# A transformer layer in five phases: the order of two interleaved stages, and the loop of an output projection, written anew

## What is computed

```python
def _layernorm(x, eps=1e-5):
    m = mean(x); v = var(x)
    return (x - m) / sqrt(v + eps)

# attention, x of 4 x 4096 x 2048, 16 heads of 128, latent size 512
q = x @ Wq + bq
kv_latent = x @ Wdown
k, v = kv_latent @ Wk_up, kv_latent @ Wv_up
q, k = rope(q), rope(k)
ctx = softmax(causal(q @ k.T / sqrt(128))) @ v
attn = ctx @ Wo + bo

x = x + _layernorm(attn(_layernorm(x)))
x = x + _layernorm(ffn(_layernorm(x)))     # ffn: silu(x Wg) * (x Wu), then Wd, int8 weights
```

## Time and profile before

| | |
|---|---|
| median of 3 runs | 6407.89 us (6402.77 to 6916.29) |
| the profiled execution: its time | 6408.3 us |
| its span, slowest core (core 4) | 6406.7 us |
| the eight cores' spans | 6387.0 to 6406.7 us |
| mean granted TensorE clock, core 4 | 0.851 |
| busy share of TensorE matmul, VectorE, ScalarE, GpSimd | 69%, 25%, 21%, 13% |

### The profile page before, as it was taken

How to read it: one execution, slowest core, us unless ns; L and a number is a source line. 1 busy time by engine, 2 the same in 40 slices (tenths; PEclk the granted TensorE clock), 3 DMA queues, 4 the chain that set the end, 5 groups by cost and what they waited for, 6 DMA issues and landing times.

```text
span 6406.7 us, 67363 instructions; the slowest of 8 cores (6387.0 to 6406.7 us)
## 1 busy us (share of the span) xinstructions
PE 4390.4 (69%) x20979; PEld 2018.1 (32%) x21376; DVE 1584.5 (25%) x2965; ACT 1347.2 (21%) x3067; POOL 819.8 (13%) x924
## 2 busy tenths in 40 slices
PE   0254544775666666533338998699986999879986
PEld 0011111333433333311113443244432444334432
DVE  0334352443333333233331110211102110021101
ACT  0222321115666666511110000001001000010000
POOL 0112121340000000000001111111111111111111
PEclk9877777886777677766669999899998999989998
DMA  9343435317777787754339994699848996499944
GB/s 184 107 124 110 124 93 135 82 57 163 151 150 147 152 154 150 146 146 135 126 105 161 154 151 129 154 151 151 148 128 158 149 154 130 127 167 155 151 122 134
DMA packets 1566328, 883.21 MB, mean 138 GB/s; under 512 B 777122, under 2 KB 1541026, under 8 KB 1550242
## 3 DMA queue, kind: packets, MB, share of 16 engines
q0 software_dynamic: 679296, 434.14, 39.6%
q1 hardware_dynamic: 839842, 327.28, 23.0%
q10 hardware_dynamic: 46848, 117.45, 5.6%
HBM read 398.53 MB, written 109.05 MB: 79 GB/s over the span
## 4 chain that ended last, share of the span: by engine, by line
PE 44%; DMA 19%; DVE 11%; ACT 10%; issue 10%; POOL 3%; SPq 2%; ACTq 1%; DVEq 0%; POOLq 0%
PE ps L1051 14%; PE ps L1065 14%; PE ps L1118 8%; DMA arena<-wd 7%; ACT arena L786 7%; PE ps L884 4%; DMA ctxr<-xin 3%; DMA arena<-arena 2%; PE ps L758 2%; DVE smalls L780 2%; POOL arena L641 2%; PE ps L719 1%; DVE arena L481 1%; DMA arena<-wo 1%; DMA x_scr<-arena 1%
## 5 line engine op out<-in xcount | busy, mean ns | idle before, releaser
L1051 PE MATMUL ps<-arena 128*128 128x512 bf16 x4015 | 929.4, 382 | 270.7 <-DMA arena<-wg 143.8
L1118 PE MATMUL ps<-arena 128*128 128x512 bf16 x4014 | 912.1, 380 | 145.1 <-DMA arena<-wd 139.8
L1065 PE MATMUL ps<-arena 128*128 128x512 bf16 x4013 | 919.7, 379 | 4.4
L786 ACT ACTIVATE arena<-ps,smalls 128x512 bf16<-128x512 f32 (+1 forms) x1152 | 748.5, 667 | 460.7 <-DVE smalls L780 314.9
L758 PE MATMUL ps<-arena 128*128 128x512 bf16 (+1 forms) x1073 | 455.0, 484 | 412.2 <-ACT arena L786 325.0
L1051 PEld LDWEIGHTS ps<-arena 128*128 128x128 bf16 x4096 | 402.7, 98 | 757.9 <-issue 281.0
L446 PE MATMUL ps<-arena 128*128 128x512 bf16 x1004 | 329.2, 472 | 397.2 <-DVE arena L481 197.5
L1118 PEld LDWEIGHTS ps<-arena 128*128 128x128 bf16 x4096 | 386.8, 98 | 669.8 <-issue 238.3
L1081 DVE TENSOR_SCALAR ctxr<-ps,smalls 128x512 bf16<-128x512 f32 x256 | 192.1, 750 | 1501.1 <-PE ps L1065 1501.1
L1065 PEld LDWEIGHTS ps<-arena 128*128 128x128 bf16 x4096 | 400.9, 98 | 483.2
L1076 ACT ACTIVATE ctxr<-ps,smalls 128x512 bf16<-128x512 f32 x256 | 176.0, 687 | 1562.5 <-PE ps L1051 1562.4
(11 more groups left out here) (74 smaller groups left out, 2742.6 us busy)
## 6 DMA issues: line engine op xcount, KB each, us to landing
arena<-wg POOLq DMA_DIRECT2D x128, 1024.0 KB, 6.8
arena<-wu POOLq DMA_DIRECT2D x128, 1024.0 KB, 7.1
arena<-wd POOLq DMA_DIRECT2D x256, 512.0 KB, 3.8
ctxr<-xin SPq DMA_DIRECT2D x32, 1024.0 KB, 6.7
arena<-wo_scr ACTq DMA_DIRECT2D x16, 2048.0 KB, 9.3
xnf_scr<-arena SPq DMA_DIRECT2D x16, 1024.0 KB, 11.8
k_scr<-ctxr SPq DMA_DIRECT2D x16, 1024.0 KB, 7.9
v_scr<-ctxr SPq DMA_DIRECT2D x16, 1024.0 KB, 7.2
```

The lines of the kernel that those rows point to most:

```text
L786: s.activation(P_b[par][:, n0:n0 + N], psa[:, 0:N], ACT.Exp, bias=negc[:, par:par + 1], scale=1.0, accum_out=lacc[:, par * 8 + ci: par * 8 ...
L1051: rr = t.matmul(ga, wg_s[slp][:, fc, icw * 128:(icw + 1) * 128], x1nfm[:, fc, :], start=(fc == 0), stop=(fc == NH - 1))
L1065: rr = t.matmul(ua, wu_s[slp][:, fc, icw * 128:(icw + 1) * 128], x1nfm[:, fc, :], start=(fc == 0), stop=(fc == NH - 1))
L1118: rr = t.matmul(psa, f_b[:, quar * 4 + ic, j * 128:(j + 1) * 128], wd_s[qp][:, ic, :], start=(quar == 0 and ic == 0), stop=(quar == 15 and ...
```

## The change

Two parts. In phase A the generators are no longer drawn in turn: for each kg the whole of `front(kg+1)` is recorded, then the whole of `back(kg)`.

In phase D Wo is loaded once, whole, into `wo_all` (four 2 MB loads at the start). The tile of 128 tokens is now the outer loop, and the four og the inner one; the row work of a tile stands right behind its four sums. `att` becomes two buffers of one tile. The transposed context `ctxfm` has one buffer instead of two: the four transposes of the next block are recorded behind the matmuls of a block's last tile. In `ln_soup` the last step, which applies scale and shift, goes from DVE to ACT, and needs a small POOL product before it (`nmr`).

```diff
-        fr = front(0)
-        run_all(fr)
-        fr = front(1) if NKG > 1 else iter(())
+        run_all(front(0))
         for kg in range(NKG):
-            bk = back(kg)
-            while True:
-                try:
-                    next(bk)
-                except StopIteration:
-                    break
-                try:
-                    next(fr)
-                except StopIteration:
-                    pass
-            run_all(fr)
-            fr = front(kg + 2) if kg + 2 < NKG else iter(())
+            if kg + 1 < NKG:
+                run_all(front(kg + 1))
+            run_all(back(kg))
...
-        ctxfm = [cd.take([NH, 512], BF16) for _ in range(2)]
-        wo_s = [cd.take([NH, 512], BF16) for _ in range(2)]
-        att = cd.take([4, DM], F32)
+        ctxfm = cd.take([NH, 512], BF16)
+        wo_all = cd.take([NH, DM], BF16)
+        att2 = [cd.take([DM], F32) for _ in range(2)]
...
+        woevs = []
+        for og in range(4):
+            def fnw(s, og=og):
...
+                return s.dma_start(wo_all[:, :, og * 512:(og + 1) * 512], sap)
+            woevs.append(st("S", fnw, dma="dA"))
+        s_wo.produced(woevs)
...
-        for ttb in range(4):
-            tp = ttb % 2
-            if ttb + 1 < 4:
-                cfm_load(ttb + 1)
-
+        for tt in range(16):
+            tp = tt % 2
+            att = att2[tp]
+            s_att = s_att2[tp]
+            j4 = tt % 4
...
             for og in range(4):
...
+                bank = og % 2
...
+            if j4 == 3 and tt + 1 < 16:
+                cfm_load(tt // 4 + 1)
...
-                    e9 = st("V", lambda v: v.tensor_scalar(
-                        dst_ap, src_ap, nmean, rstd, op0=ALU.add, op1=ALU.mult),
-                        waits=[e8] + prod_waits(sD))
+                e8b = st("G", lambda g: g.tensor_mul(nmr, nmean, rstd),
+                         waits=[e8])
+                e9 = st("S", lambda s, src_ap=src_ap, dst_ap=dst_ap:
+                        s.activation(dst_ap, src_ap, ACT.Identity,
+                                     bias=nmr, scale=rstd),
+                        waits=[e8b] + prod_waits(sD))
```

More of the change, by code:

```diff
@@ L833, in build_program @@
         bo_s = cd.take([DM], F32)
-        s_cfm = [Slot(), Slot()]
-        s_wo = [Slot(), Slot()]
-        s_att = Slot()
+        s_cfm = Slot()
+        s_wo = Slot()
+        s_att2 = [Slot(), Slot()]
         s_xt = [Slot(), Slot()]
@@ L844, in build_program @@
         s_bo.produced(st("Q", lambda q: q.dma_start(bo_s, bob), dma="dQ"))
+        woevs = []
+        for og in range(4):
+            def fnw(s, og=og):
+                sap = bass.AP(wo_scr.tensor, og * 512,
+                              [[DM, 128], [128 * DM, NH], [1, 512]])
+                return s.dma_start(wo_all[:, :, og * 512:(og + 1) * 512], sap)
+            woevs.append(st("S", fnw, dma="dA"))
+        s_wo.produced(woevs)
         def cfm_load(ttb):
-            tp = ttb % 2
             tevs = []
@@ L850, in cfm_load @@
                 tt = ttb * 4 + j
-                ev = st("Q", lambda q, tt=tt, j=j, tp=tp: q.dma_start(
-                    ctxfm[tp][:, :, j * 128:(j + 1) * 128],
+                ev = st("Q", lambda q, tt=tt, j=j: q.dma_start(
+                    ctxfm[:, :, j * 128:(j + 1) * 128],
                     ar_view(ctxr, 0, [NH, DM], BF16)[:, tt, :],
@@ L855, in cfm_load @@
                     waits=cons_waits(s_ctx) +
-                    (prod_waits(s_cfm[tp]) if j == 0 else []), dma="dQ",
+                    (prod_waits(s_cfm) if j == 0 else []), dma="dQ",
                     xpose=True)
@@ L859, in cfm_load @@
                 s_ctx.used(ev)
-            s_cfm[tp].produced(tevs)
+            s_cfm.produced(tevs)
         cfm_load(0)
-        for ttb in range(4):
-            tp = ttb % 2
-            if ttb + 1 < 4:
-                cfm_load(ttb + 1)
-            for og in range(4):
[L869 to L944, removed]
-                    e9 = st("V", lambda v: v.tensor_scalar(
-                        dst_ap, src_ap, nmean, rstd, op0=ALU.add, op1=ALU.mult),
-                        waits=[e8] + prod_waits(sD))
[L948 to L973, removed]
```

86 lines of the change are left out of this document (added).

## The result

The kernel after is slower: its time is 1.015 of that before, with a 95% interval of 1.010 to 1.021, so whether the loss reaches 2% stays open. Its profiled execution takes 6500.9 us (span 6499.4, core 3) where that of before takes 6408.3; the forecast was 6524, within 6488 to 6566. A phase starts where the table says; for D and E that is the first load that SP issues for it.

The account below looks back on a forecast made before the run. Phases A and D were taken to be bound by chains of waits, with no engine near full. From 6408.3 us, +150 for A and -34 for D gave 6524 us, 1.8% more, range 6488 to 6566.

Parts of the forecast that it names:

- Phase A, the period: Phase A: front and back add up, so the period is 131.8 us instead of 110.9, and A costs +150 us.
- if every front's first load costs more behind v than behind k: Phase A, upper bound: allows 1.7 us more per period for a front's first load behind the store of v.
- The third latent group: Phase A, back: TensorE starts this group at the low clock, 5.6 us; if warm, each period is 2.2 shorter.
- Phase D: Whole of phase D: gains from the new tile order outweigh a later start and block-end stalls, -34 us.
- start of the phase to the first reduce: Phase D, start: first matmul 15 us later behind four Wo loads, then the first tile's groups; 61.3 us in all.
- 15 pitches without stalls: Phase D, ordinary tiles: row work of 21.3 us plus matmul part of 11.6, a pitch of 32.9, 15 times.
- three stalls: Phase D, block boundaries: residual sum waits for x behind four transposes, 11 us each, 33 in all.
- extra of the first tile: Phase D, first tile: 1.3 us for the one table load.
- last row work and hand-over: Phase D, end: 21.3 us to the last reciprocal, then 5.3 to the next phase, 26.6 in all.
- TensorE stays warm: Rival, phase D: short idle stretches keep the clock up, each third group costs 3.4 us, total 6478; chance 0.10.
- DMA engines add up in D: Rival: D's start costs 25 us, boundary stalls 15 each, A at its upper bound of 162; total 6558; chance 0.30.
- The order in A is indifferent: Rival, phase A: nothing was hidden before, the period stays at 110.9 us, total 6374; chance 0.05.

Follow-up runs that it names:

- e5: The changed kernel with each load of x in phase A issued one tile ahead; 6225.5 to 6237.9 us on cores 0 to 3.
- e10: The changed kernel with loads of x in phase A issued two tiles ahead; 6194.6 us (one run).
- e8: e7, but matmuls wait only for their own fourth of Wo, and the last two Wo loads follow the first block's transposes; 6319.6 us (one run).
- e1: The kernel before with only phase A's change, phase D as before; 6555.8 to 6578.3 us, ratio 1.0235.
- e3: The kernel before with only phase D changed, plus x for a block's last tile loaded ahead of the next block's transposes; 6343.6 and 6344.1 us.
- e9: The kernel before's interleaved order in A with x loaded two tiles ahead, and D as in e8; ratio to the kernel before 0.960.
- e7: The kernel before with only phase D changed, plus each tile's x in D loaded one tile earlier; 6318.4 and 6322.2 us.

## Why the prediction was right

**Phase A, the period.** Term by term, from the period shown above: store to first load 1.1 (took 1.1); first to second load 21.1 (20.5); second to fourth 32.7 (32.7); fourth load to the end of ACT's scaling 14.6 (13.8), taking that end as 0.1 ahead of the transpose's issue; the back 63.6 (63.7). That is 133.1 instead of 131.8. Only the period behind group 0 was longer, 136.2. The claim that front and back would add up holds, and e5 and e10 show why: what the old order hid was mostly the load of x and what it waits for on SP. The step that was short is the first store of v, 2.5 us later than taken, and six periods of 1.3 more; together they are the 10 us by which group 6 came late. The allowance "if every front's first load costs more behind v than behind k" covers 0.6 of the 1.3; the other 0.8 is the fourth load, for which none was made. At +159 the phase ended inside +135 to +162, near its upper end; on the mean of the cores it is +152.

**The third latent group** starts slowly again after a front's idle time, as read from the earlier trace rows. ACT's timeline of after:

```profile
575.35 1.05 ACT L421 CAST arena<-ps 128x512 bf16<-128x512 f32 x2
582.41 0.59 ACT L421 CAST arena<-ps 128x512 bf16<-128x512 f32 x1 [6.01 <-PE ps L412]
585.87 0.59 ACT L421 CAST arena<-ps 128x512 bf16<-128x512 f32 x1 [2.87 <-PE ps L412]
```

TensorE started it at 576.17, 6.2 us before its copy (took 5.6), at a granted clock of 0.54, and the fourth took 3.5 (3.4) at 1.00.

**Phase D** gave back 63 us and not 34, still within its bounds (12 to 67). The path was the one forecast and the sizes were not; each term:

| term | forecast | measured | difference |
|---|---|---|---|
| start of the phase to the first reduce | 61.3 | 56.2 | -5.1 |
| 15 pitches without stalls | 15 x 32.9 | 15 x 31.6 | -19.5 |
| three stalls | 33 | 28.0 | -5.0 |
| extra of the first tile | 1.3 | 3.0 | +1.7 |
| last row work and hand-over | 26.6 | 26.2 | -0.4 |

The pitch is the one that counts. Its matmul part was put at 11.6 us and is 10.3 in the tile shown, 10.6 on the mean, 15 of the 19.5 us: TensorE starts the third group at 2971.24 and DVE can sum it at 2976.35, 5.1 us, where I took the 6.5 of the start of a block. The granted clock (the third number from the end; it is 1.00 at 2.4 GHz and 0.50 at 1.2) goes with it. Windows of after, the third and fourth group of that tile, and the start of the next block's first group:

```profile
2971.30:2975.70 4.40, 4.40 (x15) 1.66 (x16) 0.28 (x1) 1.63 (x1) 0.00 (x0) 0.68 0.30 119
2975.70:2980.00 4.30, 4.30 (x22) 1.94 (x21) 0.89 (x2) 0.00 (x0) 0.00 (x0) 1.00 0.00 0
3023.40:3028.00 4.60, 4.60 (x11) 1.57 (x12) 0.00 (x0) 0.00 (x0) 0.00 (x0) 0.50 0.68 235
```

A mean of 0.68 is neither level: the clock rose in the middle of the third group, and so the group cost less than the 6.5 us that went with 0.56 behind block 0 and more than the 3.4 of the rival "TensorE stays warm". How long the engine had been idle does not decide it alone. In TensorE's timeline the pair of groups takes 8.4 to 8.6 us in most tiles, after 15.5 us of idle time, but 9.7 after 12.9 at a block's end:

```profile
3002.14 8.37 PE L873 MATMUL ps<-arena 128*128 128x512 bf16 x32 [15.54 <-DVE arena L885]
3023.36 9.69 PE L873 MATMUL ps<-arena 128*128 128x512 bf16 x32 [12.85 <-DMA arena<-ctxr]
```

Ahead of the 12.9 us of idle time the engine had worked only 8.4 us since the gap before, ahead of the 15.5 us some 15. What does decide was not tested. The row work is 20.5 in the tile shown (21.0 on the mean) and not 21.3: the detour by ACT costs 1.0 where I took 0.9, but in the tiles where no load of x goes out beside it the wait for the store of x1 is 4.05 us, 0.9 less than in the tile of the earlier trace rows. What I wrote of the ACT step with an f32 output, "the bf16 one of 2.09 us is the nearest row", was right: it takes 2.09.

**D's ends.** The first matmul comes 40.0 us after the phase's start instead of 28.9, 11 more where I took 15; on the mean of the eight cores it is 39.2 instead of 26.2, 13 more. SP's timeline of after, beside the earlier trace rows:

```profile
2860.18 33.69 SPq L847 DMA_TRANSPOSE arena<-ctxr  x4
...
3011.18 9.90 SPq L847 DMA_TRANSPOSE arena<-ctxr  x4
```

Four transposes beside four loads of Wo take as long to issue as eight did beside fewer. The Trainium skill, page "DMA: Bandwidth & Descriptors", section "Issuing engines are not separate DMA queues", says that DMAs issued by different engines run on the same 16 DMA engines and interleave. The runs agree in direction: e8, with two loads fewer, starts 12 us earlier. A full sum of the two kinds, my estimate of 25 us, does not come out; its own terms, 15 + 36 less the 28.9 of before, give only 22. At a block's end the four take 9.5 to 9.9 without another load beside them, not 13, so the stall was 9.3 on the mean and not 11.

**The rivals.** *DMA engines add up in D* falls: start +11, stalls 9.3, A +159 and not +162 beside a D of -63. *TensorE stays warm* falls as stated, since the third group took 5.1 and not 3.4, but its time (6478) is as near as the forecast's: of the 46 us that it priced, some 15 did come. *The order in A is indifferent* falls with e1. The +2 in B and C and the -6 in E were not followed up; on the mean of the eight cores they are +1 and -1.

**The total.** The measured 6500.9 is 23 us below the forecast of 6524. That is partly luck: D came 28 us lower than forecast and A 9 higher, so that a part of D's miss was made up (the untouched phases came 4 lower).

## What to carry to other kernels

A phase that waits for loads may still be hiding others: before code is reordered, ask for each load what it stands behind on the engine that issues it, and whether some other work runs in that time. Here, moving the loads ahead on their queue was worth 21 us a period in the old order and 39 in the new, and made the 22 us between the two orders into 3 (the loads two tiles ahead, 111.3 to 90.3 and 132.8 to 93.6). When a wait is taken away, look at what the same engine waits for next and at what the freed transfer now runs beside: in e3, e8 and e9 that took back most of the gain.

## What the runs showed of the hardware

- The store of x1 (1 MB) is waited for 4.05 us alone (after), 4.9 to 5.5 with one load of x issued 0.5 us behind it (after, e7), and 10.4 to 12.0 with two issued just ahead of it (e3).
- Four transposes of 128 x 2048 bf16 take SP 9.5 to 9.9 us to issue alone (after, block ends), 15.3 with a load and a store of x in flight, and 33.7 beside four loads of 2 MB (after, start of D).
- A group of 16 matmuls costs 5.1 us to its sum at a granted clock of 0.68 after 15.5 us of idle time, 6.5 at 0.56 after 102 us, and 3.5 at a clock of 1.00; a gap of 12.9 us at a block's end was followed by 0.50, so the shorter gap was the dearer one (9.7 us for two groups against 8.4).
